# Four small networks in one kernel, fourth layer: the values' bias moves into VectorE's copy from PSUM, with new step lists for the last two layers

## The reference, cut to what matters

```python
# third layer, L = 16 latent channels
lat    = attention(w_theta f, w_phi f, w_g f)
sa_out = gamma_sa * (w_o lat) + f
lat2   = attention(w_theta sa_out, concepts, concepts)
out3   = gamma_moca * (w_o lat2) + sa_out
# fourth layer, on x = out3; d = 16
q = Wq x + bq ; k = Wk x + bk ; v = Wv x + bv      # 1x1 convolutions
attn = softmax(q^T k)                              # 256 x 256 for each image
out  = gamma * (v attn^T) + x
```

## Time and profile before

| | us |
|---|---|
| three runs | 115.3, 115.37, 114.19; median 115.3 |
| the profiled execution | 114.44 |
| its span, first to last instruction | 112.7 |
| around the span (114.44 - 112.7) | 1.74 |
| busy in the span: PE / DVE / ACT / POOL | 105.7 / 79.6 / 51.1 / 16.8 |
| the last two layers in the span | about 77.0 to 110.7, then the last transfer out |

### The profile page before, as it was taken

How to read it: one execution, slowest core, us unless ns; L and a number is a source line. 1 busy time by engine, 2 the same in 40 slices (tenths; PEclk the granted TensorE clock), 3 DMA queues, 4 the chain that set the end, 5 groups by cost and what they waited for, 6 DMA issues and landing times.

```text
span 112.7 us, 2152 instructions
## 1 busy us (share of the span) xinstructions
PE 105.7 (94%) x769; PEld 89.4 (79%) x769; DVE 79.6 (71%) x250; ACT 51.1 (45%) x148; POOL 16.8 (15%) x28
## 2 busy tenths in 40 slices
PE   5999989989999999989998899998999999999991
PEld 5988869858868979989996657696789998677571
DVE  1669557578899796975986444759564786688871
ACT  5151676987333243030112503014785637768760
POOL 5007996000000000000000000003300003333000
PEclk9999999999999999999999999999999999999999
DMA  3999910000000000000000000000000000000112
GB/s 78 280 370 395 435 73 6 0 0 0 3 0 0 0 3 6 0 0 0 6 0 0 0 6 0 3 0 0 0 6 0 0 0 0 0 6 0 47 53 87
DMA packets 3321, 5.24 MB, mean 47 GB/s; under 512 B 496, under 2 KB 2928, under 8 KB 3184
## 3 DMA queue, kind: packets, MB, share of 16 engines
q1 hardware_dynamic: 3168, 5.11, 13.0%
q10 hardware_dynamic: 144, 0.01, 0.1%
HBM read 4.59 MB, written 0.52 MB: 45 GB/s over the span
## 4 chain that ended last, share of the span: by engine, by line
PE 72%; DVE 13%; ACT 10%; issue 2%; DVEq 0%; ACTq 0%
PE psum L1026 11%; PE psum L1044 9%; PE psum L1110 8%; PE psum L1376 4%; PE psum L1350 4%; PE psum L1368 3%; PE psum L1151 3%; PE psum L1421 2%; PE psum L1434 2%; PE psum L1343 2%; DVE eo L658 2%; PE psum L1454 2%; PE psum L1188 2%; PE psum L1301 2%; PE psum L1358 2%
## 5 line engine op out<-in xcount | busy, mean ns | idle before, releaser
L1110 PE MATMUL psum<-spin 128*128 128x256 f32 x58 | 10.2, 330 | 1.2 <-DVE spin L582 1.2
L355 POOL TENSOR_TENSOR att_s<-xc,x 128x256 f32<-128x256 f32 x3 | 2.2, 725 | 59.5 <-DVE xc L898 59.5
L1110 PEld LDWEIGHTS psum<-spin 128*128 128x128 f32 x58 | 8.9, 228 | 1.5 <-DVE spin L582 1.2
L361 POOL TENSOR_SCALAR att_c<-x,gbv 128x256 f32<-128x256 f32 x4 | 3.8, 961 | 19.3 <-DVE x L947 19.3
L1026 PE MATMUL psum<-mixed_x,w_mix_cam 128*128 128x256 f32 x24 | 6.4, 384 | 0.0
L1026 PE MATMUL psum<-mixed_x,w_raw_cam 128*128 128x256 f32 x24 | 6.2, 379 | 0.0
L1044 PE MATMUL psum<-mixed_s,w_mix_out_s 128*128 128x128 f32 x48 | 6.2, 275 | 0.0
L1044 PEld LDWEIGHTS psum<-mixed_s,w_mix_out_s 128*128 128x128 f32 x48 | 5.9, 192 | 0.1
L1026 PE MATMUL psum<-mixed_x,w_raw_sam 128*128 128x256 f32 x24 | 5.7, 382 | 0.0
L1044 PE MATMUL psum<-mixed_c,w_mix_out_c 128*128 128x128 f32 x48 | 5.7, 275 | 0.0
L1044 PEld LDWEIGHTS psum<-mixed_c,w_mix_out_c 128*128 128x128 f32 x48 | 5.5, 192 | 0.0
(11 more groups left out here) (249 smaller groups left out, 266.3 us busy)
## 6 DMA issues: line engine op xcount, KB each, us to landing
par<-in_late SPq DMA_DIRECT2D x1, 1422.0 KB, 7.8
wide_x<-in_x SPq DMA_DIRECT2D x2, 288.0 KB, 3.9
w_raw_sam<-in_w_sam SPq DMA_DIRECT2D x3, 192.0 KB, 3.1
w_raw_cam<-in_w_cam SPq DMA_DIRECT2D x3, 192.0 KB, 4.9
w_raw_out_s<-in_w_out SPq DMA_DIRECT2D x3, 192.0 KB, 5.0
w_raw_out_c<-in_w_out SPq DMA_DIRECT2D x3, 192.0 KB, 4.9
out<-y SPq DMA_DIRECT2D x2, 128.0 KB, 1.7
out<-y SPq DMA_DIRECT2D x4, 64.0 KB, 1.5
```

What stands on the lines that cost most here:

```text
L361: nc.gpsimd.tensor_scalar(x3b[:, b, :], x3[:, b, :], gbv[:, 0:1], None, ALU.add).then_inc(ev["f_xb"], 1)
L1110: mm(bank[k][:, 0:HW], spin[:, 0:P], spin[:, :], start=True, stop=True, skip_group_check=True)
```

## The change

Four parts.

1. The constant `bv` (one column, 14th of the late ones) goes; `bv_rows`, the bias along the row and equal on all partitions (C = 128 columns), is added at the end of the packed array. The late transfer grows by 127 of its columns and the constants behind `bv` move by one column (4 bytes).
2. `gbv` and its product on DVE go (so a later wait for `prep` is for 5 instead of 6), `x3b` and POOL's four additions go, and `add_last` and `add_chunk` read `x3` itself, without the wait for `f_xb`.
3. ACT's `values3` goes; DVE's new `values_biased` takes the values from PSUM, adds `bv_rows` and writes `vt3` in one instruction for each image.
4. The three step lists of the last two layers (ACT, DVE, PE) are new orders of the same steps, but for `values3` / `values_biased`.

```diff
-            pool.wait_ge(ev["prep"], 5)
-            for b in range(B):
-                pool.wait_ge(ev["e_done"], b + 1)
-                nc.gpsimd.tensor_scalar(x3b[:, b, :], x3[:, b, :], gbv[:, 0:1], None, ALU.add).then_inc(ev["f_xb"], 1)
...
-            def values3(b):
-                act.wait_ge(ev["f_vt"], b + 1)
-                nc.scalar.copy(vt3[:, b, :], bank[2 * b + 1][:, 0:NCH * C]).then_inc(ev["f_vt_sb"], 1)
...
+            def values_biased(b):
+                dve.wait_ge(ev["f_vt"], b + 1)
+                nc.vector.tensor_tensor(vt3[:, b, :].rearrange("p (j c) -> p j c", j=NCH),
+                                        bank[2 * b + 1][:, 0:NCH * C].rearrange("p (j c) -> p j c", j=NCH),
+                                        p1("bv_rows").unsqueeze(1).broadcast_to([P, NCH, C]),
+                                        ALU.add).then_inc(ev["f_vt_sb"], 1)
...
             def add_last(b):
                 dve.wait_ge(ev["f_av"], NCH * (b + 1))
-                dve.wait_ge(ev["f_xb"], b + 1)
                 nc.vector.scalar_tensor_tensor(y[:, b, :], bank[2 * b][:, 0:HW], p1("gam3"),
-                                               x3b[:, b, :], ALU.mult, ALU.add).then_inc(ev["f_done"], NCH)
+                                               x3[:, b, :], ALU.mult, ALU.add).then_inc(ev["f_done"], NCH)
 
             def add_chunk(c):
                 b, i = divmod(c, NCH)
                 dve.wait_ge(ev["f_av"], c + 1)
-                dve.wait_ge(ev["f_xb"], b + 1)
                 nc.vector.scalar_tensor_tensor(y[:, b, P * i:P * (i + 1)], last_result(b, i), p1("gam3"),
-                                               x3b[:, b, P * i:P * (i + 1)], ALU.mult, ALU.add).then_inc(ev["f_done"], 1)
+                                               x3[:, b, P * i:P * (i + 1)], ALU.mult, ALU.add).then_inc(ev["f_done"], 1)
```

```diff
-                            (exp_concepts, 2), (queries, 0), (keys_last, 0), (values3, 0), (exp_concepts, 3),
-                            (turned_concepts, 2), (queries, 1), (exp_last, 0), (turned_concepts, 3), (values3, 1),
-                            (keys_last, 1), (keys_last, 2), (queries, 2), (values3, 2), (turned_last, 0),
-                            (exp_last, 1), (queries, 3), (values3, 3), (exp_chunk, 4), (exp_chunk, 5),
-                            (turned_last, 1), (exp_chunk, 6), (turned_chunk, 4), (exp_chunk, 7), (turned_chunk, 5),
-                            (turned_chunk, 6), (turned_chunk, 7)):
...
+                            (exp_concepts, 2), (queries, 0), (keys_last, 0), (turned_concepts, 2), (exp_concepts, 3),
+                            (keys_last, 1), (queries, 1), (turned_concepts, 3), (exp_last, 0), (queries, 2),
+                            (keys_last, 2), (exp_last, 1), (turned_last, 0), (queries, 3), (exp_chunk, 4),
+                            (turned_last, 1), (exp_chunk, 5), (turned_chunk, 4), (exp_chunk, 6), (exp_chunk, 7),
+                            (turned_chunk, 5), (turned_chunk, 6), (turned_chunk, 7)):
...
-                            (add_concepts, 1), (max_last, 0), (spread_concepts, 2), (add_concepts, 2),
-                            (normalise_last, 0), (spread_concepts, 3), (max_last, 1), (add_concepts, 3),
-                            (max_chunk, 4), (max_chunk, 5), (keys_by_dve, 3), (normalise_last, 1), (add_last, 0),
-                            (normalise_chunk, 4), (max_chunk, 6), (max_chunk, 7), (normalise_chunk, 5),
-                            (normalise_chunk, 6), (add_last, 1), (normalise_chunk, 7), (add_chunk, 4),
+                            (values_biased, 0), (add_concepts, 1), (spread_concepts, 2), (max_last, 0),
+                            (values_biased, 1), (add_concepts, 2), (spread_concepts, 3), (max_last, 1),
+                            (normalise_last, 0), (add_concepts, 3), (values_biased, 2), (normalise_last, 1),
+                            (max_chunk, 4), (max_chunk, 5), (keys_by_dve, 3), (normalise_chunk, 4),
+                            (values_biased, 3), (max_chunk, 6), (normalise_chunk, 5), (max_chunk, 7), (add_last, 0),
+                            (normalise_chunk, 6), (normalise_chunk, 7), (add_last, 1), (add_chunk, 4),
                             (add_chunk, 5), (add_chunk, 6), (add_chunk, 7)):
...
-                            (scores_last, 0), (project_last, 1), (apply_concepts, 2), (turn_concepts, 3),
-                            (values_last, 1), (out_concepts, 2), (apply_concepts, 3), (project_last, 2),
-                            (values_last, 2), (scores_last, 1), (turn_last, 0), (out_concepts, 3), (score_chunk, 4),
-                            (score_chunk, 5), (project_last, 3), (values_last, 3), (apply_last, 0), (turn_last, 1),
-                            (score_chunk, 6), (score_chunk, 7), (turn_chunk, 4), (apply_last, 1), (turn_chunk, 5),
-                            (turn_chunk, 6), (apply_chunk, 4), (apply_chunk, 5), (turn_chunk, 7), (apply_chunk, 6),
...
+                            (apply_concepts, 2), (scores_last, 0), (project_last, 1), (turn_concepts, 3),
+                            (values_last, 1), (out_concepts, 2), (apply_concepts, 3), (scores_last, 1),
+                            (project_last, 2), (values_last, 2), (out_concepts, 3), (score_chunk, 4), (turn_last, 0),
+                            (project_last, 3), (values_last, 3), (score_chunk, 5), (turn_last, 1), (apply_last, 0),
+                            (score_chunk, 6), (turn_chunk, 4), (score_chunk, 7), (apply_last, 1), (turn_chunk, 5),
+                            (apply_chunk, 4), (turn_chunk, 6), (apply_chunk, 5), (turn_chunk, 7), (apply_chunk, 6),
                             (apply_chunk, 7)):
```

More of the change, by code:

```diff
@@ L51 @@
         ("w_o_rep", C), ("w_qk3", P), ("w_v3", C),
-        ("sm_cols", WID), ("w1_cols", WID), ("sum4", WID)]
+        ("sm_cols", WID), ("w1_cols", WID), ("sum4", WID), ("bv_rows", C)]
 def columns(table):
@@ L204, in build @@
         x3 = x1
-        gbv = sb("gbv", [P, 1])
         vt3 = att_s
-        x3b = att_c
         y = sb("y", [P, B, HW])
@@ L235, in build @@
             "e_score e_max e_exp e_rinv e_tp e_pt_sb e_av e_wide e_out e_done "
-            "f_vt f_vt_sb f_q f_k f_score f_max f_exp f_rinv f_norm f_tp f_pt_sb f_av f_xb f_done").split()}
+            "f_vt f_vt_sb f_q f_k f_score f_max f_exp f_rinv f_norm f_tp f_pt_sb f_av f_done").split()}
         out_dram = out.rearrange("b c h w -> c b (h w)")
@@ L791, in _ @@
             nc.vector.tensor_scalar(gsc[:, 1:2], p1("gam_moca"), L ** -0.5, None, ALU.mult).then_inc(ev["prep"], 1)
-            nc.vector.tensor_tensor(gbv[:, :], p1("gam3"), p1("bv"), ALU.mult).then_inc(ev["prep"], 1)
             nc.vector.tensor_scalar(b1p3[:, :], p1("ca_b1", MIP), 3.0, None, ALU.add).then_inc(ev["prep"], 1)
@@ L997, in _ @@
                             (gate_rows, 2), (gate_columns, 2), (gate_rows, 3), (gate_columns, 3), (max_self, 0),
-                            (max_self, 1), (max_self, 2), (spread_self, 0), (add_self, 0), (max_self, 3),
-                            (spread_self, 1), (max_concepts, 0), (spread_self, 2), (add_self, 1), (add_self, 2),
-                            (max_concepts, 1), (spread_concepts, 0), (spread_self, 3), (add_concepts, 0),
+                            (max_self, 1), (max_self, 2), (spread_self, 0), (max_self, 3), (add_self, 0),
@@ L1001, in _ @@
+                            (spread_self, 1), (max_concepts, 0), (add_self, 1), (spread_self, 2), (max_concepts, 1),
+                            (spread_concepts, 0), (add_self, 2), (spread_self, 3), (add_concepts, 0),
                             (max_concepts, 2), (add_self, 3), (spread_concepts, 1), (max_concepts, 3),
-                            (add_concepts, 1), (max_last, 0), (spread_concepts, 2), (add_concepts, 2),
-                            (normalise_last, 0), (spread_concepts, 3), (max_last, 1), (add_concepts, 3),
@@ L1459, in _ @@
             for step, b in ((project, 0), (scores, 0), (project, 1), (project, 2), (scores, 1), (turn_self, 0),
-                            (scores, 2), (apply_self, 0), (project, 3), (turn_self, 1), (out_self, 0),
-                            (turn_self, 2), (scores, 3), (apply_self, 1), (scores_concepts, 0), (apply_self, 2),
-                            (out_self, 1), (turn_self, 3), (turn_concepts, 0), (out_self, 2), (scores_concepts, 1),
-                            (apply_concepts, 0), (apply_self, 3), (out_concepts, 0), (scores_concepts, 2),
@@ L1464, in _ @@
-                            (out_self, 3), (turn_concepts, 1), (project_last, 0), (apply_concepts, 1),
-                            (scores_concepts, 3), (values_last, 0), (out_concepts, 1), (turn_concepts, 2),
-                            (scores_last, 0), (project_last, 1), (apply_concepts, 2), (turn_concepts, 3),
-                            (values_last, 1), (out_concepts, 2), (apply_concepts, 3), (project_last, 2),
```

(13 more changed lines are left out.)

12 lines of the change are left out of this document (6 added, 6 removed).

## The result

| | before | after |
|---|---|---|
| median, us | 115.0 (114.18 to 117.01, 16 runs) | 115.71 (114.98 to 116.24, 16 runs) |
| ratio to the kernel before | | 1.0062, 95% interval 1.0037 to 1.0087 |
| the profiled execution, us (span) | 114.44 (112.7) | 116.08 (114.3) |

The account below looks back on a forecast made before the run. The prediction took the last layers to be bounded by PE's work plus 2.0 us of waits that a better order could remove. A gain of 1.2 us off 114.8 gave 113.6 us, range 112.3 to 115.4.

Parts of the forecast that it names:

- From PE's side: of the 2.0 us of waits ...: Fourth layer on PE: 0.8 of the 2.0 us of waits stays, so the gain is 1.2 us.
- 0.18 counted at 104.51: One of PE's listed waits: `turn_last` takes 0.63 us until the next start instead of 0.45.
- DVE's sum: DVE's steps from `spread_concepts` 3 to `normalise_chunk` 7 sum to 8.69 us, plus 0.1 to 0.2 of waits; gain 1.2.
- second count of the prediction: The gain counted from PE's waits and from DVE's list in the fourth layer: 1.2 us by each.
- `apply_concepts` 3 at 98.1: Fourth layer on PE: this step starts at 98.1 instead of 98.61, with a wait of about 0.1 left ahead.
- The value step at 0.42: Each of DVE's four value steps costs 0.42 us, 1.7 in all, with new waits of 0.1 to 0.3 each.
- Rival 3: DVE becomes the bound from `values_biased` 0 on: 1.7 us added less 0.6 from the order, 115.9; chance 0.07.
- Rival 2: DVE's value steps and their waits take the gain back: gain 0 to 0.3, 114.5 to 114.8 us; chance 0.29.
- Constants, POOL's additions, `f_xb`: Longer late load 0, at most 0.35 us more; dropping GpSimd's additions and the wait for them 0 directly.
- POOL's side effect on the products: Two `normalise_last` products on DVE took 0.75 us beside POOL's third addition, 0.61 without; 0.14 saved, taken as 0.
- The third layer: New order there: 0, bounds -0.3 to +0.3; the fourth layer's first projection starts within 0.1 us of before.
- The sum: Whole kernel: 114.8 - 1.2 = 113.6 us; from first `project` to last addition 32.5 us.

Follow-up runs that it names:

- e2: The kernel before, with one step of another image put between the scores of chunks 4 and 5 and of 6 and 7 on PE: ratio 1.0108 to before.
- e1: The kernel after, with the scores of chunks 4 and 5 and of 6 and 7 adjacent again in PE's list: ratio 1.0012 to before.
- e3: The kernel before, with the second score chunk of each image also reading partitions 0 to 15: ratio 1.0139 to before.
- e6: e1 with both late score pairs moved on PE, and the turn of concepts 3 and its ACT copy earlier: ratio 0.9973 to the kernel before.
- e9: The lists of e8, with values copied by ACT and `x3b` made by POOL as in the kernel before: 114.64 us, ratio 0.997 to before.
- e8: e6 with DVE's value step of image 3 moved directly behind `normalise_last` 1: 114.67 us, ratio 0.9984 to the kernel before.
- e5: The change without its new lists: old orders, with the four value steps inserted in DVE's list: ratio 1.0047 to the kernel before.
- e7: The kernel before, with `bv_rows` appended to the late constants and read by nothing: ratio 0.9991 to before.

## Why the prediction was wrong

- **The step that failed: "From PE's side: of the 2.0 us of waits ...".** It took PE's work as the same in any order, and expected the scores at "0.64" whatever stands between them. The new list splits both late pairs, which adds 1.2 us in the rows of the scores and about 0.2 beside them (the pitches after; e2 adds 1.52 by the splits alone, e1 takes 0.53 back), and e3 shows why. The rows before held the hint: four records at 105.14 with a pitch of 0.64 for all four and durations of 0.37 to 0.48 each, where two records of the same width in L1404 have a pitch of 0.54. I read 0.64 as the price of four; it was the price of two at a time. The same paragraph of the prediction also let 1.2 us of waits go, and less than that went (see the sum below). One of the "waits" was none: of the 0.18 counted at 104.51, 0.09 is the price of going from full-height to small products.
- **DVE's sum held, its waits did not.** From its first step behind `apply_concepts` 3 (99.88) to the end of the last normalisation (109.85) DVE took 9.97 us; the sum was 8.69, with 0.1 to 0.2 of waits. The two waits shown above are 1.05 of the 1.28 between them. 0.64 of that is the split itself, 0.41 is ACT's `exp_last` 1 behind the queries and keys of image 2. So the second count of the prediction did not test the first, since it took the arrival of the scores from it.
- **`apply_concepts` 3 at 98.1.** It came at 21.47 from the first `project` where 21.1 was forecast: 0.4 late. The mis-sized term is the wait "of about 0.1" that was to stay ahead of it: the four records ahead take 0.82 (98.62 to 99.44) instead of 0.45, because ACT's pair of queries and keys, 1.0 us with pitches of 0.50, stands in front of its copy of the turned concepts. Moving the turn and that copy ahead (e6) brought 21.07.
- **The value step at 0.42:** measured 0.41 to 0.42. DVE waited 0.27 and 0.33 in front of the first two, about the 0.1 to 0.3 that was allowed for.
- **Rival 3** (slower, 115.9) is nearest in time, and that is luck: it put the loss on DVE's queue from the first value step on, with no idle time left there. DVE did idle (0.27, 0.33, 0.41 and 0.64 us above), joining the pairs with all value steps left on DVE takes the loss to 0.1% (e1), and with whole pairs the engine of the values makes no difference (e9 against e8).
- **Rival 2** (the gain taken back by DVE, 0 to 0.3) has a part of truth in e5, 0.4 us for the value steps in the old order, and in e1, where two of them hold the pairs.
- **Constants, POOL's additions, `f_xb`:** for the constants 0, as said (e7). For the additions no run stands alone; before, none of DVE's add steps waited for them. POOL's side effect on the products is gone: 0.62 at both pairs of L966 after.
- **The third layer:** `project_last` 0 at 16.57 instead of 16.19, of which 0.25 is `apply_concepts` 1, which the new list puts ahead of it. The 0.38 is outside the 0.3 that the forecast allowed; without that step, which only changed places, it is 0.13.
- **The sum.** 32.5 forecast, 34.34 measured: 1.84 off. The split pairs are 1.2, and about 0.2 more in the rows beside them. The rest, 0.4 to 0.6, is waits that the forecast took as gone: `apply_concepts` 3 came 0.4 late and DVE lost 0.41 us behind ACT's exponentials, with some overlap. Joining the pairs alone gave back 0.53, joining them and mending the places that waited gave 1.1 to 1.3 (e6, e8). The last 0.6 of the forecast was reached by no run: 33.07 is the shortest tail, so what bounds these orders from there on stays open.

The version to keep is e6 or e8: 0.8 to 0.9% faster than the kernel after by the ratios. Against the kernel before they are 0.2 to 0.3% faster, with intervals that reach 1, so a gain over it is not shown.

## What to carry to other kernels

A step's price in an order written by hand is not a property of the step. Where two products lie on different rows of the array, price the pair and the lone one apart, and look for "x2 costs what x4 costs". A count of idle gaps gives an upper bound for what a new order can win, but it needs the condition that the busy part stays as long as it was. And before an engine's list is judged by busy shares, look at which pairs of steps sit back to back in it, and what each of them gains by that.

## What the hardware showed that was not expected

- Two float32 products of 16 rows by 256 columns at partitions 0 and 32 take 0.63 to 0.65 us together, one alone 0.60 to 0.65, two on the same rows 1.05 to 1.06.
- Going from full-height products to these 16-row ones and back costs about 0.3 us of PE's time: 0.09 ahead of the first, 0.10 behind it, and 0.09 ahead of the next full-height one, whose weight load comes 0.33 us behind the last small one.
- `queries` and `keys_last`, two ACT operations on 64 x 256 that read the lower and the upper 64 partitions of one PSUM bank and both write partitions 0 to 63, start 0.50 us apart in either order, though each lasts 0.47. An exponential behind `keys_last` also starts 0.50 later (101.64 to 102.14 after), behind `queries` only 0.37 (98.27 to 98.64 in e6). I did not test what holds the second back.
- The first product stretch of the kernel, the same code in all these kernels, took 2.82 to 4.06 us in ten profiled executions, enough to hide a change of this size if only two profiles are compared.
